# Attention denominators inverted once in 32 columns through 32x32 transposes, with the tables of beats moved

## The chip, the core and the metric

The kernel runs on one core of one Trainium2 chip. The metric is device microseconds (us) of one execution, lower is better. The engines are named as in the profile: PE (TensorE's matmuls), PEld (its weight loads), DVE (VectorE), ACT (ScalarE), POOL (GpSimd), SP (SyncE, whose queue here issues DMAs only).

## The reference

A gated cross-attention layer and a gated feed-forward layer on x (4 batches x 2048 tokens x 512 features), with a context of 154 rows for each batch. Cut to what matters:

```python
q, k, v = x_n @ Wq.T + bq, ctx @ Wk.T + bk, ctx @ Wv.T + bv    # x_n = layernorm(x); 16 heads of 32
att = softmax(q @ k.T / sqrt(32))                              # over the 154 context rows
y   = att @ v
x   = x + tanh(g_xattn) * (y @ Wo.T + bo)
h   = float_quantize(relu(layernorm(x) @ w1.T + b1), 4, 3)     # 2048 hidden features
out = float_quantize(h @ float_quantize(w2, 4, 3).T + float_quantize(b2, 5, 10), 5, 10)
x   = x + tanh(g_ffn) * out
```

The softmax's division is done last: PE sums the exponentials into denominators d and computes y without division; normalise() multiplies y by 1/d.

## The kernel before, in words

The 8192 tokens are 16 chunks of 512 (CHUNK), four chunks to a batch. Features or heads lie on the 128 partitions, tokens in the free dimension. A chunk passes through: query product (wq), row maxima of rough scores (`row_max`, L1013), scores and exponentials ("lift" on PE L644/L651, ACT L811/L814, POOL L1144), value product, normalise, output product with wo, residual and second layernorm, hidden product with w1, and ffn product with w2. The 16 heads are handled in four groups m of four heads. f16 operands are carried as a high and a low part: for a value y, ACT writes the high part (`y_hi`, L869) and POOL the rest (`y_lo`, L1161); likewise x2_hi (ACT L853) and x2_lo (POOL L1170).

**The order is written out by hand.** Each engine has its own program, a loop over "beats". A table gives the beat of every stage within its chunk (VALUE_AT = [7, 14, 21, 28] is the value product of groups 0 to 3); chunk c adds 28c (PERIOD). One period is 92.1 us in the steady part, so a beat is about 3.3 us, and three chunks are in the air at once: while one is in its scores, the one before is in its output and ffn products. Tables named ..._OWN give chunks 0 to 2 beats of their own, and single-line tables (WQ_LO, W1_LO, WO_LO, W2_LOAD and so on) give the beats of the weights' preparation. Within a beat the order of the `run(...)` lines fixes the order on the engine. An engine never goes out of order: each stage first waits on counting semaphores, and all behind it on that engine waits too.

**The value group.** `value` on PE writes d_ps: a matrix of ones, 32 wide, gives each head the sum of its exponentials, so the 32 rows of a head's block of partitions hold the same numbers. It then waits for the product before it to have left y_ps (semaphore y_scaled) and writes y_ps. Both are PSUM banks with one buffer: the next group's d_ps waits for `inverted`. `normalise` on DVE (L1035, L1038) does two halves of 256 columns, each a RECIPROCAL of the whole 128x256 half and a multiply into y32.

**The ring.** All products with 512-column results (wq "q", wo "o", w1 "h", w2 "f") write in turn to two PSUM banks, ring0 and ring1. A product waits until the one two before it has been moved out: q by DVE L1054, o by DVE L1077 (`residual`), h by ACT L836, f by DVE L1044 (first half of `finish`).

**From o to h.** `project` (PE, wo) is followed on DVE by `residual` (L1077, then statistics L1060, L1062), on POOL by the inverse root (L1179, L1182), on DVE by `ln2_apply` (L1086), then ACT x2_hi, POOL x2_lo and a transposing DMA into late_a, from which the hidden product reads. w1_lo, wo_lo and wq_lo (DVE L936) make the low parts of weights, 128x2048 at a time, in the first 170 us.

## Time and profile before

| | |
|---|---|
| three runs | 1588.94, 1587.31, 1587.6 us; median 1587.6 |
| the profiled execution | 1588.39 us, of which the span of the trace is 1586.6 |
| PE busy | 1533.4 us (97% of the span) |
| DVE, ACT, POOL busy | 951.8, 813.5, 877.2 us (60, 51, 55%) |
| DVE RECIPROCAL, L1035 | 223.4 us in 128 instructions |
| start-up, until PE is saturated | about 166 us |
| a steady chunk | 92.1 us |

An entry of the timeline gives start and duration; a row of PE bundles matmuls that follow each other, and [idle before <- releaser] names what ended a wait. The name in such a row is the buffer's without its number, so ring stands for both banks, w for w1 and w2, and y for y32.

### The profile page before, as it was taken

To read this page: it belongs to the slowest core of one execution; us is meant where nothing else is said; L and a number is where in the kernel's file an instruction comes from. 1 tells how busy PE (TensorE), PEld (TensorE's weight loads), DVE (VectorE), ACT (ScalarE), POOL (GpSimd) and SP (SyncE) were. 2 spreads that over 40 slices of the span, in tenths; PEclk is the share of its full clock that TensorE was granted. 3 is DMA by queue.
4 is the path that set the end of the run, shared out by engine and by line. 5 is a ranking of instruction groups with operands and counts; after the bars stand their busy time and mean duration, and the time that the engine had idled before them with its cause. 6 is when DMAs were issued, how large, how long until landed. Compare 5 with 4: busy or idle time off the path is not lost.

```text
span 1586.6 us, 23629 instructions
## 1 busy us (share of the span) xinstructions
PE 1533.4 (97%) x8600; PEld 695.7 (44%) x8600; DVE 951.8 (60%) x1297; ACT 813.5 (51%) x1196; POOL 877.2 (55%) x919
## 2 busy tenths in 40 slices
PE   7776999999999999999999999999999999999998
PEld 4322444444444444444444444444444444444443
DVE  7768665665746566574746657574665757445231
ACT  3674664645555464555546454545545455455421
POOL 3679465564746555574646547464654746445310
PEclk9988999999999999999999999999999999999999
DMA  8355464454544354354445434344543434333120
GB/s 338 94 152 150 128 157 122 134 116 112 109 139 94 117 136 113 101 114 138 104 119 132 115 103 119 115 103 131 135 114 104 120 113 104 100 100 86 44 54 27
DMA packets 252855, 186.70 MB, mean 118 GB/s; under 512 B 160012, under 2 KB 209476, under 8 KB 251076
## 3 DMA queue, kind: packets, MB, share of 16 engines
q1 hardware_dynamic: 252740, 185.19, 43.9%
q8 instruction: 69, 1.13, 0.3%
q14 instruction: 46, 0.38, 0.1%
HBM read 99.95 MB, written 51.59 MB: 96 GB/s over the span
## 4 chain that ended last, share of the span: by engine, by line
PE 73%; DVE 11%; POOL 7%; issue 4%; ACT 2%; DMA 2%; SPq 1%; DVEq 0%; ACTq 0%
PE ring L519 52%; PE ring L728 8%; PE m_ps L621 4%; DVE y L1035 3%; PE s_ps L651 2%; PE y_ps L679 2%; DVE bns L1060 2%; DVE resid L1077 2%; POOL pmain L1144 2%; POOL rs L1182 2%; DVE xn L1086 1%; PE d_ps L668 1%; POOL x L1170 1%; PE s_ps L644 1%; DMA yT<-in_wq_t 1%
## 5 line engine op out<-in xcount | busy, mean ns | idle before, releaser
L519 PE MATMUL ring<-late_a,w 128*128 128x512 f16 (+1 forms) x3096 | 703.1, 378 | 1.5 <-DMA late_a<-x 1.5
L519 PEld LDWEIGHTS ring<-late_a,w 128*128 128x128 f16 x3096 | 301.9, 98 | 338.8 <-issue 8.6
L1144 POOL TENSOR_TENSOR pmain<-p,pmain 128x512 f16<-128x512 f32 x256 | 304.3, 1191 | 173.8 <-ACT p L814 170.6
L836 ACT ACTIVATE late_b<-ring,b_sb,wsc 128x512 fp8e4<-128x512 f32 x256 | 199.3, 779 | 388.1 <-PE ring L519 388.1
L1013 DVE TENSOR_REDUCE smax<-m_ps 128x4 f32<-128x616 f32 x256 | 203.4, 794 | 229.6 <-PE m_ps L621 229.2
L1035 DVE RECIPROCAL y<-d_ps 128x256 f32<-128x256 f32 x128 | 223.4, 1745 | 58.6 <-PE d_ps L671 57.1
L814 ACT ACTIVATE p<-s_ps,prob_log,sc 128x512 f32<-128x512 f32 x320 | 247.9, 775 | 0.1
L728 PE MATMUL ring<-w,late_b 128*128 128x512 fp8e4 x1024 | 228.5, 379 | 5.4 <-DVE ffn L1044 3.8
L811 ACT ACTIVATE pmain<-s_ps,prob_log,sc 128x512 f16<-128x512 f32 x256 | 198.1, 774 | 2.7 <-PE s_ps L651 2.7
L1144 POOL TENSOR_TENSOR pleft<-p,pleft 128x512 f16<-128x512 f32 x64 | 76.9, 1201 | 183.3 <-ACT p L814 183.3
L519 PE MATMUL ring<-wo,yT 128*128 128x512 f16 x768 | 175.2, 382 | 0.0
L519 PE MATMUL ring<-xT,wq 128*128 128x512 f16 x720 | 167.5, 383 | 0.0
L728 PEld LDWEIGHTS ring<-w,late_b 128*128 128x128 fp8e4 x1024 | 97.7, 98 | 132.8 <-DVE ffn L1044 10.6
L853 ACT CAST x<-xn 128x512 f16<-128x512 f32 x64 | 39.5, 618 | 197.2 <-DVE xn L1086 197.2
L621 PE MATMUL m_ps<-kblk,qparts 128*128 128x308 f16 x512 | 112.0, 301 | 26.8 <-DVE smax L1013 25.5
L1156 POOL TENSOR_TENSOR qparts<-q,qparts 128x512 f16<-128x512 f32 x61 | 72.6, 1191 | 106.2 <-ACT qparts L860 106.2
L1054 DVE TENSOR_SCALAR q<-ring,sc,bias_s 128x512 f32<-128x512 f32 x61 | 49.3, 808 | 118.5 <-PE ring L519 114.1
L519 PEld LDWEIGHTS ring<-wo,yT 128*128 128x128 f16 x768 | 74.2, 98 | 92.9 <-issue 8.6
L519 PEld LDWEIGHTS ring<-xT,wq 128*128 128x128 f16 x720 | 71.0, 99 | 80.2 <-issue 3.6
L1044 DVE TENSOR_TENSOR ffn<-ring,bq 128x512 f16<-128x512 f32 x64 | 44.1, 688 | 99.5 <-PE ring L728 97.9
L651 PE MATMUL s_ps<-qstack,kcat 97*128 97x512 f16 x256 | 98.1, 385 | 2.9 <-ACT p L814 2.9
L1170 POOL TENSOR_TENSOR x<-xn,x 128x512 f16<-128x512 f32 x64 | 80.7, 1260 | 35.3 <-ACT x L853 35.3
(149 smaller groups left out, 1424.0 us busy)
## 6 DMA issues: line engine op xcount, KB each, us to landing
...
```

The lines of the kernel that those rows point to most:

```text
L519: last = pe.matmul(dst, lhs(a, k), rhs(b, k), start=(k == 0 and p == 0), stop=(k == n_k - 1 and p == 2))
L621: last = pe.matmul(m_ps[:, half, 0:HK], qparts[:, 0, m, t * P:t * P + P], kblk[:, m, half * HK:(half + 1) * HK], start=True, stop=True)
L651: pe.matmul(s_ps[unit(c, m, 1 + h) % 2][:], kcat[0:97, GH * m + h, 0:P], qstack[0:97, GH * m + h, :], start=True, stop=True).then_inc(lift ...
L728: last = pe.matmul(ring_bank("f", c, t)[:], hT[:, j, t * P:t * P + P], w2[:, j, :], start=(j == 0), stop=(j == HT - 1))
L811: nc.scalar.activation(dst, s_ps[n % 2][:], ACT.Exp, bias=prob_log[:, 0:1], scale=sc[:, 7:8])
L814: nc.scalar.activation(p32[:, n % 2, :], s_ps[n % 2][:], ACT.Exp, bias=prob_log[:, 0:1], scale=sc[:, 7:8]).then_inc(exped, 1)
L836: nc.scalar.activation(hT[:, j, :], ring_bank("h", c, j)[:], ACT.Relu, bias=b1_sb[:, j:j + 1], scale=wsc[:, j // 4, 1:2], saturate=False). ...
L1013: nc.vector.tensor_reduce(smax[:, m // 2, heads, t].rearrange("p (a h) -> p a h", a=2), score_view, AX.X, ALU.max).then_inc(maxed, 1)
L1035: nc.vector.reciprocal(y32[:, cols], d_ps[:, cols]).then_inc(inverted, 1)
L1144: nc.gpsimd.tensor_tensor(part[:, 1, :], p32[:, n % 2, :], part[:, 0, :], ALU.subtract).then_inc(prob_lo, 1)
L1156: nc.gpsimd.tensor_tensor(qparts[:, 1, m, :], q_stage(c, m), qparts[:, 0, m, :], ALU.subtract).then_inc(q_lo, 1)
L1170: nc.gpsimd.tensor_tensor(x2_16[:, t % 2, 1, :], xn2[:], x2_16[:, t % 2, 0, :], ALU.subtract).then_inc(x2_split, 1)
```

## The change

1. `normalise` is one call for each group, over all 512 columns. It transposes d_ps by 32x32 blocks into y32 (STREAM_TRANSPOSE). Since the 32 partitions of a block are equal, each block then has 32 equal columns; one column of each of the 16 blocks is inverted (128x16, new tile inv), broadcast 32 times and transposed back into y32, and one multiply of 128x512 follows. PE's next value product may write d_ps after the first transpose (semaphore den_turned) rather than after both reciprocals. The stage stands at one beat rather than two, behind `residual` and ahead of `finish`, and y_hi and y_lo at a beat earlier.
2. In the steady tables the output product, residual, second norm and x2's turn (O_AT, RESID_AT, LN2_AT, X2TURN_AT) stand a beat earlier.
3. Chunk 1's and 2's own tables and the weights' preparation get other beats: wq's low part goes from beat 4 to -1, the low parts of w1's four pieces from {16, 32, 26, 39} to {13, 26, 26, 38} (pieces 0, 2, 1, 3), the second shift of chunk 1 from 39 to 42, and so on.

```diff
-NORMAL_AT = [7, 8, 14, 15, 21, 22, 28, 29]
-SPLIT_Y_AT = [9, 16, 23, 30]
+NORMAL_AT = [7, 14, 21, 28]
+SPLIT_Y_AT = [8, 15, 22, 29]
...
-O_AT = [33, 34, 35, 36]
-LN2_AT = [34, 35, 36, 37]
-X2TURN_AT = [35, 36, 37, 38]
+O_AT = [32, 33, 34, 35]
+LN2_AT = [33, 34, 35, 36]
+X2TURN_AT = [34, 35, 36, 37]
...
-W1_LO = {0: 16, 1: 26, 2: 32, 3: 39}
+W1_LO = {0: 13, 1: 26, 2: 26, 3: 38}
...
+        inv = sb("inv", [P, CHUNK // DH], F32)
...
                 if g:
-                    pe.wait_ge(inverted, 2 * g)
+                    pe.wait_ge(den_turned, g)
...
                 if g:
-                    pe.wait_ge(y_scaled, 2 * g)
+                    pe.wait_ge(y_scaled, g)
...
             def y_hi(c, m):
-                act.wait_ge(y_scaled, 2 * group(c, m) + 2)
+                act.wait_ge(y_scaled, group(c, m) + 1)
...
-            def normalise(c, k):
-                m, half = divmod(k, 2)
-                g, cols = group(c, m), slice(half * HALF_COLS, (half + 1) * HALF_COLS)
-                if half == 0:
-                    dve.wait_ge(den_done, g + 1)
-                    if g:
-                        dve.wait_ge(y_lo_done, g)
-                    else:
-                        dve.wait_ge(q_lo, KT)
-                nc.vector.reciprocal(y32[:, cols], d_ps[:, cols]).then_inc(inverted, 1)
-                dve.wait_ge(inverted, 2 * g + half + 1)
+            def normalise(c, m):
+                g = group(c, m)
+                dve.wait_ge(den_done, g + 1)
+                if g:
+                    dve.wait_ge(y_lo_done, g)
+                else:
+                    dve.wait_ge(q_lo, KT)
+                nc.vector.transpose(y32[:], d_ps[:]).then_inc(den_turned, 1)
+                dve.wait_ge(den_turned, g + 1)
+                nc.vector.reciprocal(inv[:], y32[:].rearrange("p (b j) -> p b j", j=DH)[:, :, 0]).then_inc(inverted, 1)
+                dve.wait_ge(inverted, g + 1)
+                nc.vector.transpose(y32[:], inv[:].unsqueeze(2).to_broadcast([P, CHUNK // DH, DH])).then_inc(spread, 1)
+                dve.wait_ge(spread, g + 1)
                 dve.wait_ge(valued, g + 1)
-                nc.vector.tensor_tensor(y32[:, cols], y_ps[:, cols], y32[:, cols], ALU.mult).then_inc(y_scaled, 1)
+                nc.vector.tensor_tensor(y32[:], y_ps[:], y32[:], ALU.mult).then_inc(y_scaled, 1)
...
                 run(shift, SHIFT_AT, beat, SHIFT_OWN)
-                run(normalise, NORMAL_AT, beat)
                 run(ln2_apply, LN2_AT, beat, LN2_OWN)
...
                 run(residual, O_AT, beat, O_OWN)
+                run(normalise, NORMAL_AT, beat)
                 run(finish, FFN_AT, beat, FFN_OWN)
```

What this does to the engines' order is shown at three places. Line numbers of the changed kernel are two to four higher than those of before.

First, PE where a steady chunk's output products (wo) stand around the first value product of the next chunk. Before:

```order
L519 MATMUL ring1<-wo,yT 128x512 x12
L519 MATMUL ring0<-wo,yT 128x512 x12
L644 MATMUL s_ps1<-qstack,kcat 32x512 x4
L668 MATMUL d_ps<-pmain,ones 32x512 x8
L671 MATMUL d_ps<-pstack,ones_stack 32x512 x4
L679 MATMUL y_ps<-pmain,vmain 32x512 x12
L683 MATMUL y_ps<-pstack,vstack 32x512 x4
L519 MATMUL ring1<-wo,yT 128x512 x12
L651 MATMUL s_ps0<-qstack,kcat 128x512
L519 MATMUL ring0<-wo,yT 128x512 x12
L651 MATMUL s_ps1<-qstack,kcat 128x512
L728 MATMUL ring1<-w2,late_b 128x512 x16
```


After the change, from the same place on (a row `s_ps1`, the second lift, and the first ffn product in ring1 follow):

```order
L521 MATMUL ring0<-wo,yT 128x512 x12
L521 MATMUL ring1<-late_a,w1 128x512 x12
L623 MATMUL m_ps<-kblk,qparts 128x308 x2
L521 MATMUL ring0<-wo,yT 128x512 x12
L521 MATMUL ring1<-wo,yT 128x512 x12
L646 MATMUL s_ps1<-qstack,kcat 32x512 x4
L670 MATMUL d_ps<-pmain,ones 32x512 x8
L673 MATMUL d_ps<-pstack,ones_stack 32x512 x4
L681 MATMUL y_ps<-pmain,vmain 32x512 x12
L685 MATMUL y_ps<-pstack,vstack 32x512 x4
L521 MATMUL ring0<-wo,yT 128x512 x12
L653 MATMUL s_ps0<-qstack,kcat 128x512
```


The first output product has moved ahead of the last hidden product, the third ahead of the value product, and only the fourth is left between the value product and the ffn products; both single lifts now follow it.

Second, DVE at the same place, from the group's denominators to the last `ln2_apply` (xn2). Before:

```order
L1035 RECIPROCAL y32<-d_ps 128x256
L1038 TENSOR_TENSOR y32<-y_ps,y32 128x256
L1086 TENSOR_SCALAR xn2<-resid,mv2,rs2 128x512
L1077 SCALAR_TENSOR_TENSOR resid<-ring1,sc,resid 128x512
L1060 BN_STATS bns<-resid 128x6
L1062 BN_AGGR mv2<-bns 128x2
L1035 RECIPROCAL y32<-d_ps 128x256
L1038 TENSOR_TENSOR y32<-y_ps,y32 128x256
L1086 TENSOR_SCALAR xn2<-resid,mv2,rs2 128x512
L1077 SCALAR_TENSOR_TENSOR resid<-ring0,sc,resid 128x512
L1060 BN_STATS bns<-resid 128x6
L1062 BN_AGGR mv2<-bns 128x2
```

After, from the third `ln2_apply` to `finish`:

```order
L1090 TENSOR_SCALAR xn2<-resid,mv2,rs2 128x512
L1081 SCALAR_TENSOR_TENSOR resid<-ring0,sc,resid 128x512
L1064 BN_STATS bns<-resid 128x6
L1066 BN_AGGR mv2<-bns 128x2
L1035 STREAM_TRANSPOSE y32<-d_ps 128x512
L1037 RECIPROCAL inv<-y32 128x16
L1039 STREAM_TRANSPOSE y32<-inv 128x512
L1042 TENSOR_TENSOR y32<-y_ps,y32 128x512
L1090 TENSOR_SCALAR xn2<-resid,mv2,rs2 128x512
L1048 TENSOR_TENSOR ffn16<-ring1,bq2 128x512
L1051 SCALAR_TENSOR_TENSOR resid<-ffn16,sc,resid 128x512
```

The two half reciprocals stood one before the third and one before the last residual; the turned form stands whole behind the last residual and its statistics, just ahead of the last `ln2_apply` and of `finish`.

Third, DVE in the start-up, at the low parts of w1 (L936) around a normalise of chunk 0. Before:

```order
L936 SCALAR_TENSOR_TENSOR w1<-late_a,wsc,w1 128x2048
L1013 TENSOR_REDUCE smax<-m_ps 128x4
L1054 TENSOR_SCALAR q32<-ring0,sc,bias_s 128x512
L1070 TENSOR_SCALAR xin<-xin,mv1,rs1 128x512
L1035 RECIPROCAL y32<-d_ps 128x256
L1038 TENSOR_TENSOR y32<-y_ps,y32 128x256
L1013 TENSOR_REDUCE smax<-m_ps 128x4
L1035 RECIPROCAL y32<-d_ps 128x256
L1038 TENSOR_TENSOR y32<-y_ps,y32 128x256
```

After:

```order
L938 SCALAR_TENSOR_TENSOR w1<-late_a,wsc,w1 128x2048
L938 SCALAR_TENSOR_TENSOR w1<-late_b,wsc,w1 128x2048
L1015 TENSOR_REDUCE smax<-m_ps 128x4
L1058 TENSOR_SCALAR q32<-ring0,sc,bias_s 128x512
L1074 TENSOR_SCALAR xin<-xin,mv1,rs1 128x512
L1035 STREAM_TRANSPOSE y32<-d_ps 128x512
L1037 RECIPROCAL inv<-y32 128x16
L1039 STREAM_TRANSPOSE y32<-inv 128x512
L1042 TENSOR_TENSOR y32<-y_ps,y32 128x512
L1015 TENSOR_REDUCE smax<-m_ps 128x4
```

The row maximum that stood between the halves now follows the whole normalise, and the product for piece 2 of w1 (late_b), which before came some fifteen rows later, is ahead of it and of a row maximum.

## Rows read from the trace of the kernel before

**Rows 1.** Windows of the span: busy us of each engine (instructions), granted clock, DMA share, GB/s.

```profile
90.00:166.00 76.00, 52.44 (x278) 21.85 (x277) 61.57 (x70) 40.26 (x57) 60.45 (x56) 0.80 0.55 145
...
280.00:372.10 92.10, 91.81 (x532) 41.64 (x528) 56.93 (x76) 48.22 (x73) 53.51 (x57) 1.00 0.49 122
```

**Rows 2.** Waits over the whole span: us in total, times, longest.

```profile
PE m_ps L621 <- DVE smax L1013: 25.5, 12, 5.5
...
PEld ring L728 <- DVE resid L1077: 5.7, 14, 0.6
...
PE ring L728 <- DVE ffn L1044: 3.8, 13, 0.3
```

**Rows 3.** Timeline of PE, a steady chunk's end: start, us, what [idle before].

```profile
423.25 3.62 PE L728 MATMUL ring<-w,late_b 128*128 128x512 fp8e4 x16
426.70 0.38 PE L651 MATMUL s_ps<-qstack,kcat 97*128 97x512 f16 x1
427.07 3.63 PE L728 MATMUL ring<-w,late_b 128*128 128x512 fp8e4 x16
430.53 0.38 PE L651 MATMUL s_ps<-qstack,kcat 97*128 97x512 f16 x1
431.21 1.47 PE L728 MATMUL ring<-w,late_b 128*128 128x512 fp8e4 x6 [0.29 <-DVE ffn L1044]
```

**Rows 4.** Timeline of DVE, the same stretch.

```profile
419.15 1.74 DVE L1035 RECIPROCAL y<-d_ps 128x256 f32<-128x256 f32 x1
...
423.43 1.72 DVE L1035 RECIPROCAL y<-d_ps 128x256 f32<-128x256 f32 x1
...
426.27 0.74 DVE L1077 SCALAR_TENSOR_TENSOR resid<-ring,sc,resid 128x512 f32<-128x512 f32 x1
...
429.18 1.37 DVE L1086 TENSOR_SCALAR xn<-resid,mv,rs 128x512 f32<-128x512 f32 x1 [1.23 <-POOL rs L1182]
430.47 0.68 DVE L1044 TENSOR_TENSOR ffn<-ring,bq 128x512 f16<-128x512 f32 x1
```

**Rows 5.** Sources on DVE: count, ns min/median/max, first and last start, forms.

```profile
L1035 DVE RECIPROCAL y<-d_ps x128: 1723/1747/1758, 70.9 to 1489.3; 128x256 f32<-128x256 f32 x128
...
L1038 DVE TENSOR_TENSOR y<-y_ps,y x128: 423/424/426, 72.7 to 1491.0; 128x256 f32<-128x256 f32 x128
...
L925 DVE STREAM_TRANSPOSE amax<-fold_a x2: 211/211/211, 22.3 to 59.5; 128x32 f32<-128x32 f32 x2
...
L932 DVE RECIPROCAL rp<-pw x2: 176/182/189, 23.6 to 60.8; 128x3 f32<-128x3 f32 x1, 128x5 f32<-128x5 f32 x1
...
L1019 DVE TENSOR_SCALAR neg<-smax x32: 148/504/1175, 46.2 to 1424.6; 128x32 f16<-128x32 f32 x32
...
L1024 DVE STREAM_TRANSPOSE negT<-neg x32: 211/211/214, 46.4 to 1425.1; 128x32 f16<-128x32 f16 x32
```

**Rows 6.** Timelines of ACT and POOL in the steady stretch of rows 3.

```profile
426.91 0.77 ACT L811 ACTIVATE pmain<-s_ps,prob_log,sc 128x512 f16<-128x512 f32 x1
...
428.25 0.61 ACT L869 CAST yT<-y 128x512 f16<-128x512 f32 x1
...
429.12 1.15 POOL L1144 TENSOR_TENSOR pmain<-p,pmain 128x512 f16<-128x512 f32 x1
```

**Rows 7.** Timeline of PE, tail.

```profile
1511.94 4.26 PE L728 MATMUL ring<-w,late_b 128*128 128x512 fp8e4 x19 [0.58 <-DVE resid L1077]
```

**Rows 8.** Timeline of PE in the start-up.

```profile
113.72 0.46 PE L621 MATMUL m_ps<-kblk,qparts 128*128 128x308 f16 x2 [1.24 <-DVE smax L1013]
...
128.58 0.67 PE L621 MATMUL m_ps<-kblk,qparts 128*128 128x308 f16 x2 [3.43 <-DVE smax L1013]
...
157.55 0.67 PE L621 MATMUL m_ps<-kblk,qparts 128*128 128x308 f16 x2 [4.43 <-DVE smax L1013]
```

**Rows 9.** Source of DVE's long products of weight preparation.

```profile
L936 DVE SCALAR_TENSOR_TENSOR w<-late_b,wsc,w x1: 2686/2686/2686, 135.5 to 135.5; 128x2048 f16<-128x2048 f32 x1
L936 DVE SCALAR_TENSOR_TENSOR w<-w,wsc x1: 3287/3287/3287, 161.6 to 161.6; 128x2048 f16<-128x2048 f32 x1
```

More of the change, by code:

```diff
@@ L57 @@
 VALUE_AT = [7, 14, 21, 28]
-NORMAL_AT = [7, 8, 14, 15, 21, 22, 28, 29]
-SPLIT_Y_AT = [9, 16, 23, 30]
+NORMAL_AT = [7, 14, 21, 28]
+SPLIT_Y_AT = [8, 15, 22, 29]
 RELOAD_AT = [28, 29, 30, 31]
-RESID_AT = [30, 31, 32, 33]
-O_AT = [33, 34, 35, 36]
-LN2_AT = [34, 35, 36, 37]
-X2TURN_AT = [35, 36, 37, 38]
-HIDDEN_HALVES = {0: 39, 1: 40, 2: 41, 3: 41}
+RESID_AT = [29, 30, 31, 32]
+O_AT = [32, 33, 34, 35]
+LN2_AT = [33, 34, 35, 36]
+X2TURN_AT = [34, 35, 36, 37]
+HIDDEN_HALVES = {0: 40, 1: 40, 2: 41, 3: 42}
 HIDDEN_AT = [41, 42, 43, 45, 47, 49, 51, 52, 53, 54, 55, 56, 57, 58, 59, 60]
@@ L73 @@
 MAX_OWN = {0: [-12, -11, -10, -9, -8, -7, -6, -5, -4, -3, -2, -1, 0, 1, 2, 3], 1: [18, 19, 20, 21, 22, 23, 24, 25, 27, 29, 30, 30, 33, 34, 38, 39], 2: [46, 47, 48, 49, 50, 51, 52, 53, 54, 55, 56, 57, 58, 59, 60, 61]}
-SHIFT_OWN = {0: [-4, 4], 1: [26, 39], 2: [53, 61]}
-LN1_STAT_OWN = {1: [0, 3, 3, 6]}
-LN1_APPLY_OWN = {1: [1, 6, 9, 10]}
-XSPLIT_OWN = {1: [4, 7, 10, 11]}
-XTURN_OWN = {1: [6, 10, 14, 16]}
-Q_OWN = {1: [16, 17, 21, 27], 2: [44, 46, 50, 51]}
-STACK_OUT_OWN = {1: [19, 30], 2: [46, 53]}
-STACK_IN_OWN = {1: [24, 33], 2: [48, 59]}
-SPLIT_Y_OWN = {0: [12, 16, 24, 30]}
-RELOAD_OWN = {0: [18, 23, 28, 34]}
-RESID_OWN = {0: [29, 33, 34, 35]}
+SHIFT_OWN = {0: [-4, 4], 1: [26, 42], 2: [53, 61]}
+LN1_STAT_OWN = {1: [-1, 1, 3, 5]}
+LN1_APPLY_OWN = {1: [1, 4, 6, 7]}
+XSPLIT_OWN = {1: [3, 7, 11, 11]}
+XTURN_OWN = {1: [5, 10, 15, 15]}
+Q_OWN = {1: [16, 17, 21, 27], 2: [44, 46, 48, 50]}
+STACK_OUT_OWN = {1: [19, 27], 2: [48, 52]}
+STACK_IN_OWN = {1: [21, 31], 2: [49, 53]}
+SPLIT_Y_OWN = {0: [12, 16, 25, 30]}
+RELOAD_OWN = {0: [19, 23, 25, 28]}
+RESID_OWN = {0: [27, 32, 33, 35]}
 O_OWN = {0: [33, 35, 36, 37]}
@@ L87 @@
 HIDDEN_OWN = {0: [41, 42, 43, 45, 47, 49, 51, 52, 53, 54, 55, 56, 57, 58, 59, 60]}
-FFN_OWN = {0: [65, 66, 67, 67]}
-STORE_OWN = {0: [66, 69, 70, 72]}
+FFN_OWN = {0: [65, 66, 67, 68]}
+STORE_OWN = {0: [66, 67, 68, 69]}
 X2TURN_OWN = {0: [36, 39, 39, 39]}
-KV_STEPS = {4: [-4, -4, -3, -3], 5: [-1, 1, 1, 2], 6: [3, 5, 5, 6], 7: [5, 5, 6, 7], 8: [8, 9, 9, 10], 9: [9, 10, 10, 11], 10: [11, 11, 12, 12], 11: [14, 15, 15, 16], 12: [18, 18, 18, 19]}
+KV_STEPS = {4: [-4, -4, -3, -2], 5: [-1, 1, 1, 2], 6: [3, 5, 5, 6], 7: [5, 5, 6, 7], 8: [8, 8, 9, 9], 9: [9, 10, 10, 11], 10: [11, 12, 12, 12], 11: [14, 15, 15, 16], 12: [18, 19, 19, 19]}
 Q_STEPS = {2: [-12, -11, -10, -9], 3: [-8, -7, -6, -5]}
-KSTACK_AT = {0: -12, 1: -12, 2: -11, 3: -9, 4: -8, 5: -7, 6: -6, 7: -5}
-KEYS_OUT_AT = {0: 16}
-GATE_AT = {0: -7}
-BIAS_AT = {0: -4}
-W1_SUM = {1: -8, 2: -4, 3: -3}
-WQ_HI = {0: 0}
-WQ_LO = {0: 4}
+KSTACK_AT = {0: -12, 1: -11, 2: -10, 3: -9, 4: -8, 5: -7, 6: -6, 7: -5}
+KEYS_OUT_AT = {0: 21}
+GATE_AT = {0: -4}
+BIAS_AT = {0: -3}
+W1_SUM = {1: -9, 2: -7, 3: -2}
+WQ_HI = {0: -8}
+WQ_LO = {0: -1}
 W_FOLD = {0: 1}
-WO_HI = {0: 14}
+WO_HI = {0: 15}
 WO_LO = {0: 18}
-W1_HI = {0: 12, 1: 20, 2: 23, 3: 30}
-W1_LO = {0: 16, 1: 26, 2: 32, 3: 39}
-W2_LOAD = {0: 28, 1: 44, 2: 47, 3: 55}
-W2_PART = {0: 39, 1: 49, 2: 51, 3: 56}
+W1_HI = {0: 11, 1: 20, 2: 24, 3: 30}
+W1_LO = {0: 13, 1: 26, 2: 26, 3: 38}
+W2_LOAD = {0: 27, 1: 47, 2: 49, 3: 53}
+W2_PART = {0: 43, 1: 49, 2: 52, 3: 56}
 def build(nc, x, ctx_t, g_xattn, g_ffn, wq_t, bq, wk_t, bk, wv_t, bv, wo_t, bo, w1_t, b1, w2_t, b2, out):
@@ L244, in build @@
         lifted, exped, prob_lo = sem("lifted"), sem("exped"), sem("prob_lo")
-        den_done, inverted = sem("den_done"), sem("inverted")
+        den_done, den_turned, inverted, spread = sem("den_done"), sem("den_turned"), sem("inverted"), sem("spread")
         valued, y_scaled, y_hi_done, y_lo_done = sem("valued"), sem("y_scaled"), sem("y_hi_done"), sem("y_lo_done")
```

## The prediction, made before the changed kernel was run

> **What bounds the kernel now.** I first read the windows. In a steady chunk PE is busy 91.81 of 92.10 us at full granted clock, with DVE, ACT and POOL at 48 to 57 [rows 1]: there PE's work is the bound, and a cheaper DVE instruction is worth only the gap that it closes. In 90 to 166 us PE is busy 52.44 of 76.00, at a granted clock of 0.80, and DVE (61.57) and POOL (60.45) are the busiest: there DVE time can be time. Then the waits: what PE waits for most is DVE's row maximum, 25.5 us in 12 waits. Next come DVE's evictions ahead of the ffn products, 13 or 14 times: once in every steady chunk [rows 2]. The timeline shows this small gap. After the lift of 426.70 the second ffn product could start at 426.70 + 0.22 = 426.92 and starts at 427.07 (0.15 lost). After the lift of 430.53 the third could start at 430.75 and starts at 431.21 (0.46 lost) [rows 3]. (0.22 is the step at 2.4 GHz from one 512-column matmul to the next: 16 ffn matmuls take from 423.25 to 426.70, 3.45/16.) Together 0.61 us a chunk. I take it that 13 chunks do this.
>
> Why DVE is late there: its timeline, ahead of the eviction at 430.47, holds two half normalises (reciprocals at 419.15 and 423.43), each just before work that PE's ring needs. The last residual, which empties the bank of the second ffn product, runs at 426.27 though its product had ended before 423.25. The last ln2_apply, pushed behind it by the statistics and POOL, ends at 430.5, and only then does the first ffn product's bank get emptied [rows 3, 4].
>
> **The normalise, priced.** Before, a group costs 2 x (1.747 + 0.424) = 4.34 us of DVE [rows 5]. After, there are four instructions, of which no row of before has the size. The multiply of 128x512: an addition of that size from PSUM takes 0.68 [rows 4]. The inversion of 128x16: the short reciprocals of 3 and 5 columns take 0.18; with (1.747 - 0.182)/252 = 6.2 ns a further column, 16 columns take 0.25 [rows 5]. The transposes: 32 columns take 0.211, in f32 and f16 alike [rows 5]. Lower bound: 0.21 + 480 columns at the multiply's slope, (0.68 - 0.424)/256 = 1.0 ns, is 0.69. Upper bound: all 0.21 is paid for each of 16 blocks, 3.4. I take 0.7, since 0.15 to 0.2 is what even the smallest DVE instruction shows, so that the 0.21 is mostly a fixed part. Sum 0.7 + 0.25 + 0.7 + 0.68 = 2.35 us, 2.0 less than before; bounds 2.3 and 7.7.
>
> A row that could speak against this: the shift's small TENSOR_SCALAR swings from 148 to 1175 ns, but the transpose right behind it keeps to 211 to 214 in all 32 cases [rows 5]. So something holds the one and has not held the other, though POOL has 1.15 us instructions all about [rows 6]. By the Trainium skill ("SBUF — State Buffer", section on the two separate sides) DVE in a two-port mode and GpSimd take a shared port pair as an exclusive lock, and the loser is blocked for the other's whole instruction. If the second transpose, which goes from SBUF to SBUF, fell under it, a normalise would be up to 1.15 dearer, 3.5 us; by the rows of the 32 small transposes it stays at 2.35. The trace agrees with the rule for TENSOR_SCALAR and shows no held transpose.
>
> **The steady part.** The order shows two things. PE's third output product now ends before the value product, so that DVE's third residual is long done, and the last residual need only follow the last output product, which ends at about 422.8 (two lifts at 0.22 lie between it and 423.25). No normalise stands before it. It runs at 422.9 to 424.6 at the latest (an ln2_apply of up to 1.0 us may be ahead) against a need at 426.92: the 0.15 is gone, with over 2 us in hand. Then, on DVE: statistics 0.9 (to 425.5), the normalise 2.35 (to 427.8), ln2_apply 0.55 to 1.4 (to 428.4 to 429.2), eviction of the first ffn product 0.68 (to 429.1 to 429.9). It is needed at 430.75: the 0.46 is gone as well, with 0.9 to 1.6 in hand. All other PE work is the same in kind and count. Gain: 13 x 0.61 = 8.0 us. It can't be more than this from this cause; PE is otherwise full.
>
> The next thing that could be late is ACT: y_hi (0.61) now waits for the whole normalise at about 427.8 and stands an exp pair earlier, ahead of an x2_hi and of the exps that ran at 426.91 [rows 6]. I take this as covered, but it is the first rival.
>
> **The tail.** The last chunk has no value products after it. Its third or last residual holds the ffn product at 1511.94: 0.58 us [rows 7]. With the output products a beat earlier this falls away: 0.6.
>
> **The start-up** (five normalises of chunks 0 and 1 before PE is full). I put no term for a clock that changes. Place by place:
> - 91 to 103 us: a low part of w1 moves earlier, away from a row maximum; a short wait of PE for that maximum goes: +1.
> - 106 to 117: row maxima stand between and behind half normalises; waits such as 1.24 at 113.72 [rows 8]. 2.0 us of DVE go, PE is paced by ACT as well in part: +1.5.
> - 119 to 133: PE waits 3.43 at 128.58 [rows 8]. The 2.69 us product for late_b [rows 9] now stands ahead of this row maximum, which it delays, while the maximum no longer stands between halves. About even, up to 1 lost here; but the same 2.69 us and one 2.0 us are gone from the stretch 133 to 157, which ends in PE's wait of 4.43 at 157.55 [rows 8].
> - 157 to 167: the last 3.29 us product [rows 9] now stands ahead of a row maximum and the second shift of chunk 1, which SP must carry to the next lift. It takes back most of what 133 to 157 gave. Counted together: +1.5.
> - wq's low part at beat -1: a product of the kind of [rows 9], moved to where PE has slack on one side and a row maximum on the other; taken as 0.
>
> Sum +4. Bounds: the worst is both low parts charged in full, less a saved normalise, 2.69 - 2.0 + 3.29 = 4.0 lost. The best is all five normalises' 2.0 on PE's path, less 1 that DVE idled: 9 gained.
>
> **Sum.** 8.0 + 0.6 + 4 = 12.6. The profiled execution (1588.39) would take 1575.8. The median of the runs lies 0.8 below that execution, so I predict 1575 us.
>
> **Rivals.**
> 1. *ACT's new place for y_hi eats the steady gain.* ACT waits until 427.8, then y_hi 0.61, x2_hi 0.6, which itself waits for the last ln2_apply (428.4 to 429.2), and the two exps of 0.77 that free the bank of the lift of 430.53 [rows 3, 6]. They end between 429.8 and 431.3, against a need at about 430.5: 0 to 0.9 us a chunk lost instead of 0.61. For it: everything on ACT waits in order, and the new wait is for four instructions. Against it: the middle of the estimates has it just in time. At 0.6 a chunk only tail and start-up are left: 1587.6 - 4.6, about 1583.
> 2. *The start-up gives more.* Each us that DVE is earlier in 106 to 157 carries, as the row maxima's 25.5 us are mostly there. A gain of 10: 1569. Against it: both low parts now stand before row maxima.
> 3. *The transposes are dear: slower.* The margin of 0.9 to 1.6 behind the normalise is used up if it costs over 3.3 to 4.0 us; at 2 x 0.46 us more than the gap is back, so that it decides from some 1.3 us per transpose on. If each is held for one POOL instruction (0.7 + 1.15 = 1.85), the normalise is 4.65, the eviction ends at 431.4 to 432.2, and 0.7 to 1.4 us a chunk are lost instead of 0.61: 0 to +10 us, and the start-up's gain is gone: about 1594. At 3.4 each (7.7) it is 4.5 to 5 a chunk, over 1635. Against it: no transpose of the trace took over 0.214 us. Only the second held, once: a normalise of 3.5, the eviction at 430.3 to 431.1, 0 to 0.35 us a chunk lost, a gain of 3 to 8 in the steady part, about 1579. (The lock of the page named above, if it took in transposes, would do this second thing.)
> 4. *No change.* The gap of 0.61 returns as another wait (rival 1 in full), and the start-up's reordered low parts cost the 4 they might bring: 1587.
>
> **How the numbers follow.** Forecast (steady gap closed, start-up 0 to 8): 0.50, its own range 1571 to 1580. Rival 1: 0.20 (1580 to 1585). Rival 2: 0.12. Rival 3: 0.09. Rival 4: 0.09. 0.2% is 3.2 us, about what a measurement can tell from no change of this kernel. Faster than 1584.4: 0.50 + 0.12 + most of rival 1 = 0.80; within: 0.11; slower than 1590.8: 0.09. The range runs from the start-up's better half (1587.6 - 8.6 - 9 = 1570, and 3 lower, since a DVE that is ahead also starts the weights' preparation and the DMAs behind it earlier, which the bound of 9 leaves out) to rival 1's and part of rival 4's end: 1567 to 1586.5.
>
> **What would show it.** Right: in a steady chunk no wait of an ffn product for DVE, a chunk of 91.5 us in place of 92.1, STREAM_TRANSPOSE of 128x512 at 0.7 us, normalise instructions summing to 2.35, the waits for row maxima down from 25.5 to about 20. Wrong: transposes over 1.3 us; a wait of a lift for ACT's exps at the end of each chunk; a start-up (until PE is full) not near 162 us; waits at the shift or the lift behind the last low part of w1.

## The result, and the profile after

The changed kernel takes 1583.34 us (median of 10 runs, 1581.32 to 1586.63), the kernel before 1587.34 (10 runs, 1586.45 to 1588.94): ratio 0.9975, 95% interval [0.9965, 0.9984]. It is faster by 4.0 us, where 12.6 were forecast: the time lies in the forecast's range of 1567 to 1586.5, the gain is a third of it. The profiled execution took 1584.49 us with a span of 1582.7, against 1588.39 and 1586.6, so that its traces differ by 3.9 us.

The windows of the kernel after, in the start-up and in a steady chunk, answer to [rows 1]:

```profile
90.00:166.00 76.00, 49.97 (x279) 21.26 (x281) 51.73 (x69) 39.48 (x56) 59.45 (x56) 0.80 0.55 151
...
280.00:372.10 92.10, 92.10 (x532) 41.88 (x531) 47.47 (x76) 48.33 (x72) 53.63 (x56) 1.00 0.46 122
```

PE is now busy the whole of the steady chunk (92.10 of 92.10). DVE has dropped from 56.93 to 47.47 us: 7.9 of the 9.5 are the four normalises, the rest other DVE instructions that ran shorter. Almost nothing of it is time. In the start-up DVE is down from 61.57 to 51.73 and PE still does less in the same 76 us (49.97 against 52.44). The granted clock is 0.80 in both windows, but not in their parts: in 90 to 140 us it was 0.76 before and is 0.80 after, in 140 to 166 us it was 0.87 and is 0.80.

The sources of the four instructions of the normalise on DVE (against [rows 5]):

```profile
L1035 DVE STREAM_TRANSPOSE y<-d_ps x64: 697/707/717, 72.7 to 1483.9; 128x512 f32<-128x512 f32 x64
...
L1037 DVE RECIPROCAL inv<-y x64: 252/254/255, 73.4 to 1484.7; 128x16 f32<-128x16 f32 x64
...
L1039 DVE STREAM_TRANSPOSE y<-inv x64: 711/711/712, 73.7 to 1485.0; 128x512 f32<-128x512 f32 x64
...
L1042 DVE TENSOR_TENSOR y<-y_ps,y x64: 691/691/693, 74.5 to 1485.7; 128x512 f32<-128x512 f32 x64
```

0.71 + 0.25 + 0.71 + 0.69 = 2.36 us, with minimum and maximum within 0.02 of the median in 64 cases each. The prediction's price was 2.35.

The waits over the whole span (against [rows 2]):

```profile
PE m_ps L623 <- DVE smax L1015: 22.6, 14, 4.8
...
PEld ring L521 <- DVE resid L1081: 6.0, 14, 0.4
...
PE ring L730 <- ACT late_b L838: 0.9, 1, 0.9
```

The 13 waits of ffn products for DVE are gone, and so is the tail's wait of [rows 7]. The waits for row maxima went from 25.5 to 22.6 us only.

The timelines of PE and DVE at the place of [rows 3, 4]; the value product now stands later in the order, so that this place comes a little later in the span:

```profile
425.12 0.60 PE L653 MATMUL s_ps<-qstack,kcat 97*128 97x512 f16 x2
425.55 3.62 PE L730 MATMUL ring<-w,late_b 128*128 128x512 fp8e4 x16
429.01 0.38 PE L653 MATMUL s_ps<-qstack,kcat 97*128 97x512 f16 x1
429.23 3.62 PE L730 MATMUL ring<-w,late_b 128*128 128x512 fp8e4 x16
```

```profile
425.69 0.74 DVE L1081 SCALAR_TENSOR_TENSOR resid<-ring,sc,resid 128x512 f32<-128x512 f32 x1
...
427.30 0.70 DVE L1035 STREAM_TRANSPOSE y<-d_ps 128x512 f32<-128x512 f32 x1
...
429.67 0.54 DVE L1090 TENSOR_SCALAR xn<-resid,mv,rs 128x512 f32<-128x512 f32 x1
430.14 0.68 DVE L1048 TENSOR_TENSOR ffn<-ring,bq 128x512 f16<-128x512 f32 x1
```

PE goes from the two lifts at 425.12 to the first ffn product (425.55), 3.46 us later to the lift and 0.22 us later to the second ffn product, without a gap. The last residual (425.69) frees its bank at 426.43, 2.8 us ahead of 429.23. The first ffn product's bank is empty at 430.82; the third ffn product will need it at 432.91.

**Where the time came from.** The two traces can be laid on each other at the value products, whose start is PE's row L668 (L670 after). Value product 5 is chunk 1, group 1, and so on. At 5 the changed order has put half a hidden product (1.28 us) behind this place, which the last column takes out; at the other places here PE has the same work behind it.

| value product | before, us | after, us | after less before | same work |
|---|---|---|---|---|
| 0 | 70.03 | 69.72 | -0.31 | -0.31 |
| 2 | 102.12 | 99.52 | -2.60 | -2.60 |
| 4 | 140.40 | 137.46 | -2.94 | -2.94 |
| 5 | 167.06 | 165.65 | -1.41 | -0.13 |
| 7 | 209.04 | 208.96 | -0.08 | -0.08 |
| 9 | 256.76 | 259.38 | +2.62 | +2.62 |
| 13 | 348.87 | 351.05 | +2.18 | +2.18 |
| 17 | 441.03 | 442.72 | +1.69 | +1.69 |
| 21 | 533.12 | 534.38 | +1.26 | +1.26 |
| 61 | 1453.58 | 1450.92 | -2.66 | -2.66 |
| end of span | 1586.6 | 1582.7 | -3.9 | -3.9 |

So the changed kernel was 2.9 us ahead at 140 us, about as forecast to this point, lost 2.8 between 140 and 167, lost 2.7 more between 209 and 259, and then gained 0.43 to 0.49 in each of the chunks shown, 5.3 to value product 61, and 1.2 behind it: 0.7 in the tail, near the forecast's 0.6, and 0.5 that was not foreseen (PE's wait for POOL ahead of value product 62, 1.14 us before, is 0.62).

The loss between value products 4 and 5 can be read off PE row by row:

| PE between value products 4 and 5 | before, us | after, us |
|---|---|---|
| a lift's wait for ACT's p | 1.82 | 2.15 |
| wait for a row maximum | 4.43 | 4.78 |
| first 24 matmuls of a hidden product | 4.62 | 5.29 |
| wait for late_a | 1.49 | 1.78 |
| a lift's wait for the shift rows | none | 1.16 |

Together 12.36 and 15.16, the 2.8 us. Rows after, of PE and of DVE, and the one of DVE before that answers to the latter:

```profile
155.26 0.67 PE L623 MATMUL m_ps<-kblk,qparts 128*128 128x308 f16 x2 [4.78 <-DVE smax L1015]
155.73 5.29 PE L521 MATMUL ring<-late_a,w 128*128 128x256 f16 x24
...
165.44 0.40 PE L646 MATMUL s_ps<-qstack,kcat 97*32 97x512 f16 x4 [1.16 <-DMA qstack<-negT]
```

```profile
151.46 1.37 DVE L1090 TENSOR_SCALAR xn<-resid,mv,rs 128x512 f32<-128x512 f32 x1 [2.84 <-POOL rs L1186]
```

```profile
153.75 1.37 DVE L1086 TENSOR_SCALAR xn<-resid,mv,rs 128x512 f32<-128x512 f32 x1 [1.47 <-POOL rs L1182]
```

The row maximum stands on DVE behind this ln2_apply, the next residual and its statistics. DVE is idle ahead of it in both kernels, waiting for POOL's inverse root, so that time saved on DVE doesn't shorten PE's wait here. The experiments below tell what lengthened it.

The loss between 209 and 259 us is PE's wait of 2.52 us at 226.35 and 0.53 at 220.85, less the chunk's usual gain. Timelines of ACT, POOL, DVE and PE there:

```profile
216.37 1.91 ACT L803 ACTIVATE w<-resid 128x2048 fp8e4<-128x2048 f32 x1 [1.44 <-DMA resid<-in_w_t]
...
219.51 0.61 ACT L871 CAST yT<-y 128x512 f16<-128x512 f32 x1
...
220.80 1.15 POOL L1165 TENSOR_TENSOR yT<-y,yT 128x512 f16<-128x512 f32 x1
221.91 1.27 POOL L1180 TENSOR_TENSOR resid<-resid,gbo 128x512 f32<-128x512 f32 x1
...
223.54 0.55 POOL L1186 TENSOR_TENSOR rs<-rs,minus_half 128x1 f32<-128x1 f32 x1
...
224.13 1.37 DVE L1074 TENSOR_SCALAR xin<-xin,mv,rs 128x512 f32<-128x512 f32 x1 [6.12 <-POOL rs L1186]
...
226.35 0.42 PE L623 MATMUL m_ps<-kblk,qparts 128*128 128x308 f16 x2 [2.52 <-DVE smax L1015]
```

ACT waits 1.44 us for the load of w2's last piece and converts it for 1.9. y_hi (219.51) comes late behind that. POOL has y_lo (220.80) and a reload's addition, and only then the inverse root of chunk 3's first norm (223.54). DVE waits 6.12 us for that root, and the row maximum that frees m_ps stands behind it. In the kernel before, ACT converted this piece without a wait (215.16), and y_lo stood behind this inverse root (220.00 the root, 221.63 y_lo).

### The profile page after: what moved, and what is told of

Its sections match the earlier page's. It is cut to its first block, busy times and chain, and to the rows that moved or that the text cites. A ratio compares the mean times of both kernels' runs of the same rounds, so it can differ in the third digit from the quotient of the medians.

```text
span 1582.7 us, 23565 instructions
## 1 busy us (share of the span) xinstructions
PE 1530.0 (97%) x8600; PEld 695.8 (44%) x8600; DVE 805.9 (51%) x1297; ACT 814.3 (51%) x1196; POOL 879.5 (56%) x919
## 4 chain that ended last, share of the span: by engine, by line
PE 91%; POOL 3%; DVE 2%; DMA 1%; ACT 1%; issue 1%; SPq 0%; ACTq 0%; DVEq 0%
PE ring L521 61%; PE ring L730 14%; PE m_ps L623 4%; PE s_ps L653 3%; PE y_ps L681 3%; PE d_ps L670 2%; PE s_ps L646 1%; POOL pmain L1148 1%; PE y_ps L685 1%; PE d_ps L673 1%; DMA yT<-in_wq_t 1%; PE ring L581 1%; POOL yT L1165 0%; DVE w L938 0%; POOL qparts L1160 0%
## 5 line engine op out<-in xcount | busy, mean ns | idle before, releaser
L623 PE MATMUL m_ps<-kblk,qparts 128*128 128x308 f16 x512 | 112.6, 302 | 26.5 <-DVE smax L1015 22.6
L1169 POOL TENSOR_TENSOR x<-xin,x 128x512 f16<-128x512 f32 x60 | 71.6, 1194 | 49.8 <-ACT x L847 49.8
L862 ACT CAST qparts<-q 128x512 f16<-128x512 f32 x61 | 37.7, 618 | 114.1 <-DVE q L1058 114.1
```

The costliest lines, as they stand in the source:

```text
L623: last = pe.matmul(m_ps[:, half, 0:HK], qparts[:, 0, m, t * P:t * P + P], kblk[:, m, half * HK:(half + 1) * HK], start=True, stop=True)
L1169: nc.gpsimd.tensor_tensor(x16[:, t % 2, 1, :], xin[:, t, :], x16[:, t % 2, 0, :], ALU.subtract).then_inc(x_split, 1)
```

## The experiments

Each was timed against the kernel before in the same set of runs on one chip (medians of 1587.2 to 1587.6 us). "Form" is the turned normalise, "steady tables" are those for all chunks, "start tables" the ..._OWN ones and those for the weights.

**The form alone.** The kernel before with the changed `normalise` and its semaphores; tables and order of before, the whole normalise at the beat and place of the old second half.

```diff
-NORMAL_AT = [7, 8, 14, 15, 21, 22, 28, 29]
+NORMAL_AT = [8, 15, 22, 29]
```

> Only the turned normalise on the tables of before (whole at the beat and the place of the old second half). Theory A, the steady gain comes from DVE's shorter chain whatever the order: DVE is 4.34 - 2.35 = 2 us earlier at the last residual and at the ffn eviction, 0.6 us a chunk are closed, and a start-up without the new tables gains 0 to 4: 1576 to 1581. Theory B, it is the new order that closes the gap: 1584 to 1588, with DVE waits of about 0.5 us ahead of the ffn products still there.

Measured: 1586.40 us (11 runs), ratio 0.999 [0.9982, 0.9999]. Theory B: the steady gap is all there, and value products 9 to 57 are as far apart as before to 0.1 us. The trace is 2.7 us ahead at value product 5, all that the form alone gives, where the medians of the runs differ by 1.2 only. Timelines of DVE and PE in the same chunk as [rows 3, 4] (some 3 us earlier in the span):

```profile
413.19 1.48 DVE L1090 TENSOR_SCALAR xn<-resid,mv,rs 128x512 f32<-128x512 f32 x1 [0.72 <-POOL rs L1186]
...
417.51 1.37 DVE L1090 TENSOR_SCALAR xn<-resid,mv,rs 128x512 f32<-128x512 f32 x1 [1.23 <-POOL rs L1186]
...
422.78 0.55 DVE L1090 TENSOR_SCALAR xn<-resid,mv,rs 128x512 f32<-128x512 f32 x1
...
426.15 1.37 DVE L1090 TENSOR_SCALAR xn<-resid,mv,rs 128x512 f32<-128x512 f32 x1 [1.23 <-POOL rs L1186]
427.44 0.68 DVE L1048 TENSOR_TENSOR ffn<-ring,bq 128x512 f16<-128x512 f32 x1
...
427.50 0.38 PE L653 MATMUL s_ps<-qstack,kcat 97*128 97x512 f16 x1
428.18 1.68 PE L730 MATMUL ring<-w,late_b 128*128 128x512 fp8e4 x7 [0.29 <-DVE ffn L1048]
```

The counterpart of 417.51 in the kernel before:

```profile
421.36 0.55 DVE L1086 TENSOR_SCALAR xn<-resid,mv,rs 128x512 f32<-128x512 f32 x1
```

DVE is 2 us a group lighter and idles where it had no wait before: 1.23 us ahead of the ln2_apply at 417.51, and 1.23 at 426.15 as before, each time for POOL's inverse root. The last ln2_apply ends at the same place relative to PE as before, the eviction is at 427.44 and PE loses its 0.46 us at 428.18. From the first of the four ln2_apply to the last are 12.96 us, and were 13.05. The first and the last of these three steps are set by a round: ln2_apply, x2_hi on ACT, x2_lo on POOL, inverse root on POOL (in order behind x2_lo), next ln2_apply (417.51 - 413.19 = 4.3 us and 426.15 - 422.78 = 3.4). In the middle step the whole normalise still holds the ln2_apply at 422.78, 0.8 us behind the end of POOL's root (421.92). And the ln2_apply at 417.51 takes 1.37 us where its counterpart took 0.55. So what the shorter normalise saves comes back as waits in the round and as a longer ln2_apply.

**The tables alone.** The new kernel with the old reciprocals and multiplies, both halves one after the other at the new place.

```diff
-NORMAL_AT = [7, 14, 21, 28]
+NORMAL_AT = [7, 7, 14, 14, 21, 21, 28, 28]
```

> The new tables and the new place, with the old reciprocals and multiplies (both halves one after the other at the new beat). Theory A: the normalise of 4.34 us stands ahead of the last ln2_apply and the ffn eviction, which comes at 431 to 432 where 430.75 is needed: 0.3 to 1.2 us a chunk, and the start-up loses: 1588 to 1598. Theory B: faster than before, 1580 to 1584.

Measured: 1611.11 us (5 runs), ratio 1.015 [1.0136, 1.0164]. Slower, as theory A had it, by more than its range, and by another wait. Timelines of ACT and PE:

```profile
436.93 0.62 ACT L869 CAST yT<-y 128x512 f16<-128x512 f32 x1 [3.87 <-DVE y L1038]
437.45 0.61 ACT L853 CAST x<-xn 128x512 f16<-128x512 f32 x1
...
439.46 0.39 PE L651 MATMUL s_ps<-qstack,kcat 97*128 97x512 f16 x1 [1.34 <-ACT p L814]
```

ACT waits 3.87 us for the normalise, then comes x2_hi and only then the exponentials; PE's lift waits 1.34 us for them in each chunk. It is the mechanism of rival 1, with the 4.34 us normalise: PE waits for ACT's p 23.2 us in 16 times. With y at its new beat the new tables need the short form.

**The output stages alone a beat earlier**, with old reciprocals at their old beats, once with the new HIDDEN_HALVES and once without.

```diff
-RESID_AT = [30, 31, 32, 33]
-O_AT = [33, 34, 35, 36]
-LN2_AT = [34, 35, 36, 37]
-X2TURN_AT = [35, 36, 37, 38]
+RESID_AT = [29, 30, 31, 32]
+O_AT = [32, 33, 34, 35]
+LN2_AT = [33, 34, 35, 36]
+X2TURN_AT = [34, 35, 36, 37]
```

> The kernel before with the output product, residual, second norm and x2's turn a beat earlier, and the old reciprocals at their old beats. Theory A, the steady gap is closed by this order alone, whatever the normalise costs: 1580 to 1583, a steady period of 91.6 to 91.7 us. Theory B, order and short normalise are both needed: 1586 or more, with another wait in each chunk in place of the old one.

> The kernel before with only the output stages a beat earlier and the hidden halves where they were. Theory A, the later hidden halves cost 1.2 us in the start-up (the wait for the shift rows at 167 us): 1582 to 1583. Theory B, they cost nothing: 1583.8, as with them moved.

Measured: 1583.78 us (10 runs), ratio 0.9977 [0.9968, 0.9986], and 1583.18 (5 runs), 0.9964 [0.995, 0.9977]. The first is 0.8 above theory A's range, but its mechanism is there: the order closes the gap with the old form, and a steady chunk is about 0.55 us shorter. The second pair of theories isn't told apart by the runs (0.6 us), but by the profiles: with the new halves a lift waits 1.07 us for the shift rows at 167.60, with the old ones it doesn't. It is the same between the new kernel (1.16 us at 165.44) and the one with the halves alone put back (below; no such wait): half a hidden product less stands ahead of this lift. Two steady windows of the latter run:

```profile
280.00:372.10 92.10, 92.10 (x532) 42.08 (x531) 55.67 (x77) 48.17 (x72) 54.16 (x57) 1.00 0.48 121
372.10:464.20 92.10, 91.63 (x530) 41.67 (x528) 55.57 (x77) 48.18 (x72) 53.32 (x57) 1.00 0.45 117
```

The first is full, the second has lost 0.47: there PE waits for a row maximum at 405.91. It is the only steady chunk that does, and with the short form and y at the old beats none does. This wait is all that the short form is worth in the steady part, once the order is right. As much speed as the whole change has (4.0 us) comes from moving four stages by a beat.

**The new kernel with the old start tables.**

> The new kernel with the tables of before for chunks 0 to 2 and the weights. Theory A, the new start-up tables cost about 3 us (the stall at 220 to 226 us): 1578 to 1581 and no PE wait for the row maximum there. Theory B, they gain and the new y place costs: 1584 to 1588.

Measured: 1585.08 us (11 runs), ratio 0.9981 [0.9973, 0.999]. In theory B's range: the stall for a row maximum is there all the same (1.76 us at 225.59), so the start tables alone don't cause it. The new kernel has 1.7 us less, but the intervals of the two ratios overlap: that the new start tables gain isn't shown here, only that they cost no 3 us.

**w2's loads and conversions at the old beats**, in the new kernel.

> The new kernel with only the loads and conversions of w2 at the beats of before. Theory A, the stall at 220 to 226 us comes from ACT's conversion of w2's last piece, whose load lands late (8.1 us): with it gone 1580 to 1581, and the runs lie closer together. Theory B, it comes from y_lo standing a beat earlier on POOL, ahead of an inverse root: the stall of 2 to 3 us stays, 1583.

Measured: 1592.42 us (6 runs), ratio 1.003 [1.0018, 1.0041]. Both theories missed by 9 us and more: the stall of 2.52 stayed (at 236.55), and the old beats brought a new one. Nor could the run tell the two theories apart, since of the last piece it moves only the load (beat 53 to 55): the conversion stands at beat 56 in both tables, and ACT still waited 1.39 us for the load. SP and PE:

```profile
196.01 0.35 SPq L466 DMA_DIRECT2D resid<-in_w_t  x1
...
212.37 2.55 SPq L396 DMA_DIRECT2D qstack<-negT  x4
...
216.31 0.62 PE L646 MATMUL s_ps<-qstack,kcat 97*32 97x512 f16 x4 [4.89 <-DMA qstack<-negT]
```

The shift rows (qstack<-negT) are sent at 212.37, where the new kernel sends them at 202.83, since SP stood from 173 us on at the load of w2's third piece, which must wait until ACT has converted the second (194.09 to 195.99) and is issued at 196.01, with the stacking of q queued behind it. PE waits 4.89 us for the shift rows. The trace is 10.2 us longer than the new kernel's, 5.3 more than this wait. The granted clock is 0.70 in 160 to 172 us and 0.51 in 215 to 222, where the new kernel has 0.96 and 1.00; how the 5.3 divide isn't shown. The load's old beat (47, the conversion's is 49) fits only with the old places of SP's other work.

**y a beat later**, for chunk 1's last group only, and throughout.

```diff
-SPLIT_Y_OWN = {0: [12, 16, 25, 30]}
+SPLIT_Y_OWN = {0: [12, 16, 25, 30], 1: [36, 43, 50, 58]}
```

> The new kernel with one entry changed: y of chunk 1's last group is split a beat later, as before. Theory A, the stall of 2.5 us at 226 us is POOL's inverse root behind this y_lo: 1580 to 1581, no PE wait for the row maximum at 220 to 230 us. Theory B, it is ACT's conversion of w2: 1583 to 1584, the wait stays.

> The new kernel with y_hi and y_lo at the steady beats of before (9, 16, 23, 30). Theory A, the earlier y place is no part of the gain: the same steady period of 91.7 us or 0.1 less, and the stall at 226 us gone as well: 1579 to 1581. Theory B, the earlier y is needed by the output products: slower than the new kernel, 1584 or more.

Measured: 1580.80 us (5 runs), ratio 0.9962 [0.995, 0.9974], and 1582.23 (5 runs), 0.9963 [0.9951, 0.9974]. The first has theory A's time, though a wait stays; the second is 1.2 above its theory A's range and nearer to it than to theory B. POOL in the first of them:

```profile
219.33 0.55 POOL L1186 TENSOR_TENSOR rs<-rs,minus_half 128x1 f32<-128x1 f32 x1
...
220.97 1.33 POOL L1165 TENSOR_TENSOR yT<-y,yT 128x512 f16<-128x512 f32 x1
```

The inverse root (219.33) is now ahead of y_lo (220.97), and PE's wait of 2.52 is one of 0.93. Not all of the difference is y's place, since in this profile ACT didn't wait for w2's last load either. The profiles side by side:

| kernel | y of this group | ACT's wait for the load | PE's wait for the row maximum |
|---|---|---|---|
| before; the form alone | old beat | none | none |
| y later for one group; y later throughout; the fastest (below) | old beat | none | 0.93; 0.92; 0.93 |
| the fastest with w1's old beats (below) | old beat | 0.97 | 1.92 |
| new kernel, old start tables | new beat | none | 1.76 |
| halves alone put back (below); new kernel | new beat | 1.17; 1.44 | 2.52; 2.52 |

So 0.9 us come with the new steady tables whatever y does, 0.8 with y's new beat and 0.8 to 1.0 with a late load (the wait of 0.53 us at 220.85 is in the profiles with a late load and y at its new beat only). No experiment says why it is late in some kernels and not in others (in the new kernel it lands 8.1 us after its issue, in the run with one entry changed 6.1).

y's place costs at 148 to 155 us as well. There the lift's wait for p and the wait for the row maximum are 6.9 us together in the three profiles with y at the new beat and the new start tables, and 5.4 to 5.7 in the three with y at the old one: 1.3 us. On POOL y_lo (148.25) stands ahead of x2_lo and the inverse root (150.88) that the ln2_apply at 151.46 waits for. The other half of the story is what doesn't change: the wait for the row maximum there is 4.42 or 4.43 us before, with the form alone, with the order alone and in the fastest, whatever a normalise costs.

In every steady chunk of the new kernel y's place works in the same way, but less. Timelines of POOL, DVE and PE:

```profile
404.14 1.16 POOL L1165 TENSOR_TENSOR yT<-y,yT 128x512 f16<-128x512 f32 x1
...
406.87 0.55 POOL L1186 TENSOR_TENSOR rs<-rs,minus_half 128x1 f32<-128x1 f32 x1
...
407.46 1.37 DVE L1074 TENSOR_SCALAR xin<-xin,mv,rs 128x512 f32<-128x512 f32 x1 [2.79 <-POOL rs L1186]
...
409.33 0.38 PE L653 MATMUL s_ps<-qstack,kcat 97*128 97x512 f16 x1
409.69 0.42 PE L623 MATMUL m_ps<-kblk,qparts 128*128 128x308 f16 x2
```

y_lo at 404.14, inverse root at 406.87, DVE waits 2.79, and the product of the rough scores (m_ps) starts 0.36 us after the lift where 0.22 is the step: 0.14 lost. With y at the old beats throughout a chunk gains 0.54 to 0.62 on the kernel before, not 0.43 to 0.49.

**Sums.** The new kernel in all three. The first has the start tables of before with the normalise of chunks 0 and 1 at beat 8 and so on, and y of these chunks at its old beats; the second also puts y and hidden halves back; the third has in addition the normalise at beat 8 throughout.

```diff
-NORMAL_AT = [7, 14, 21, 28]
+NORMAL_AT = [8, 15, 22, 29]
```

> New normalise and new steady tables; the start-up tables of before, and in chunks 0 and 1 normalise and y at their beats of before (8 and 9, and so on). If start-up and steady part add up, the start-up gives the 2.9 us of the normalise alone and the steady part 0.49 a chunk and 0.6 in the tail: 1587.5 - 2.9 - 6.9 = 1577.7. If they don't add up, the stall for the row maximum comes back in the start-up: 1581 to 1585.

> Steady tables of the new kernel but y at the beats of before and the hidden halves at the beats of before; start-up tables of before, normalise of chunks 0 and 1 at their old second-half beats. Theory A, start-up gain of the short normalise (2.3 us) and steady gain (0.57 a chunk, as with the later y) add up: 1587.4 - 2.3 - 7.4 - 0.6 = 1577 to 1579. Theory B, the steady tables cost 2 to 3 us in the start-up whatever y does: 1580 to 1582.

> As the run before it, but the normalise at the second-half beat (8, 15, 22, 29) throughout, behind the residual of its beat. Theory A, the place of normalise within a beat or two is free once it is short: within 1 us of the run before it. Theory B, the shorter way from the normalise to y_hi costs ACT time and PE waits for exponentials: 2 us or more slower than that run.

Measured: 1582.41 us (5 runs), ratio 0.9968 [0.9957, 0.998]; 1580.63 (5 runs), 0.9952 [0.9939, 0.9964]; and 1596.76 (5 runs), 1.0055 [1.0041, 1.0069]. The first and second add up only in part, 2 to 5 us short of the sum. Both sums took the form's gain in the start-up (2.9 and 2.3 us) from single traces, while its runs give 1.2. The third showed "the place is free once the normalise is short" to be false: 16 us for one beat. Its waits:

```profile
PE m_ps L623 <- DVE smax L1015: 35.7, 26, 5.5
...
PEld ring L730 <- DVE ffn L1048: 9.1, 14, 0.7
```

The ffn waits are back (the normalise is again ahead of the first eviction and behind the last ln2_apply), and one wait for a row maximum a chunk has been added (26 in place of 13), 0.79 us in a steady chunk, the maximum standing directly behind the normalise.

**New start tables, y and hidden halves at the old beats.** The new kernel with the two lines put back.

```diff
-SPLIT_Y_AT = [8, 15, 22, 29]
+SPLIT_Y_AT = [9, 16, 23, 30]
-HIDDEN_HALVES = {0: 40, 1: 40, 2: 41, 3: 42}
+HIDDEN_HALVES = {0: 39, 1: 40, 2: 41, 3: 41}
```

> The new kernel with y_hi and y_lo at the steady beats of before and the hidden halves at theirs. Theory A, the new start-up tables are worth 1 to 2 us, the later y 3 us: 1579 to 1580.5. Theory B, the new start-up tables are worth nothing or less: 1582 and slower than the first run of this set.

Measured: **1578.64 us** (5 runs, 1576.20 to 1580.88), ratio 0.994 [0.9927, 0.9953]. This is the fastest, 8.5 us under the kernel before and 4.7 under the changed one, and a little below theory A's range. The parts seen above are of this size: y's place 0.13 us in each of 12 steady chunks (1.6), 0.8 at 226 us and 1.3 at 148 to 155, the later halves 1.1, together 4.8 (an estimate from single traces). Against the sum with the old start tables (1580.63) the new start tables have 2.0 us less, with overlapping intervals.

**The hidden halves alone, and w1's parts at the old beats** in that fastest version.

> The new kernel with only the hidden halves at the beats of before. Theory A, the later halves cost the new kernel 1 to 3 us in 157 to 175 us (half a product less ahead of the wait for the shift rows, and a low clock behind it): 1580.5 to 1582.5. Theory B, all of the 4.7 us between the new kernel and the run with later y and old halves are the y place: 1583 to 1584.

> The fastest version so far (new kernel, y and hidden halves at the beats of before) with the high and low parts of w1 at the beats of before. Theory A, the low parts moved ahead of row maxima cost time, as the prediction had it: 1575 to 1577. Theory B, moving them ahead is a gain, since DVE is then free for the rows behind: 1579.5 to 1583. No difference: within 1 us of 1578.6.

Measured: 1582.18 us (7 runs), ratio 0.9966 [0.9954, 0.9977], and 1579.62 (5 runs), 0.9947 [0.9934, 0.996]. The first lies in the range of theory A, but 1.2 us under the new kernel is within what runs scatter: the medians don't settle it. Its profile has no wait for the shift rows. The second: no difference that 5 runs show. The low parts moved ahead of row maxima neither cost nor give more than about a microsecond.

## Why the prediction was wrong

- **The price of the normalise** (2.35 us, 2.0 saved a group) was right: 2.36. The transposes at 0.7 were right, and POOL held none of them: 697 to 717 and 711 to 712 ns in 64 cases each. The lock in the Trainium skill ("SBUF — State Buffer", the two separate sides) is stated there for DVE in a two-port mode or with two SBUF inputs, and names no transpose; by this trace it doesn't reach these.
- **The start-up** (+4) is the step that failed: up to value product 9 the trace lost 3.1 us (2.6, and a chunk's gain of 0.5 is already in it). Up to 140 us it was about right. The +1.5 for the stretch behind it rested on DVE's lighter load shortening PE's wait of 4.43 us for a row maximum. That wait isn't made by DVE's work but by the round through ACT and POOL: it stays at 4.42 or 4.43 with the short form, and is 4.78 in the changed kernel.
- **Two table entries got no term at all.** y a beat earlier was looked at on ACT alone; on POOL it stands ahead of an inverse root, and that costs about 3.7 us (1.6 in the steady chunks, 0.8 and 1.3 in the start-up). The later hidden halves aren't in the prediction; they cost the 1.1 us wait for the shift rows. With both put back the kernel is 4.7 us faster. The stretch 209 to 259 us was taken as free of changes because PE is busy there; but the inverse root of the next chunk's norm, y_lo and w2's last load and conversion meet in it.
- **The steady part** (8.0) had the right place and too large a size: both waits of the ffn products are gone, 0.61 us a chunk, but 0.43 to 0.49 arrive, 5.8 in all (5.3 and the first chunk's 0.5). Most of the rest is the new wait of 0.14 behind y_lo.
- **The reason given for the gap** (two half normalises, "each just before work that PE's ring needs") was wrong in its weight. With the form alone the gap stays, with the order alone it closes. Of [rows 4] the prediction read the two reciprocals and named POOL only in passing; the 1.23 us for POOL's inverse root at 429.18 were the sign of the round.
- **The tail** (0.6): right.
- **The low parts of w1**, which set the lower bound of the start-up: no difference could be told. A sign of being wrong that the prediction named, a wait behind the last low part of w1, did come (1.16 us at 165.44), but not from it: with the halves put back and the low part where it is, the wait is gone.
- **Rival 1** (ACT) named the right engine for the old form (1.34 us a chunk, seen with the tables alone) and not for the new one: y_hi at 429.79 delays no lift. That its figure of about 1583 us is the measured one is luck.

Sum of the profiled execution: +2.6 at value product 9, -5.3 in the steady part and -1.2 behind it: -3.9, against -12.6. Of the 8.7 us between them the start-up has 7.1 and the steady part 2.2; 0.5 came unforeseen the other way.

What stays open in 140 to 167 us is the time of the hidden products and the wait for late_a, about 1 of the 2.8 us. The first 24 matmuls took 4.62 us at a granted clock of 0.59 before and 5.29 at 0.52 after. How much that varies is seen in the fastest version and in the one with w1's old beats, whose programs differ little there. PE's hidden products after the wait for late_a read:

```profile
160.86 2.78 PE L521 MATMUL ring<-late_a,w 128*128 128x256 f16 x24 [3.47 <-DMA late_a<-x]
```

```profile
161.48 5.28 PE L521 MATMUL ring<-late_a,w 128*128 128x256 f16 x24 [3.62 <-DMA late_a<-x]
```

and the windows 160 to 168 us of the two:

```profile
160.00:168.00 8.00, 7.14 (x68) 4.25 (x69) 2.37 (x4) 4.23 (x6) 1.54 (x2) 1.00 0.18 56
```

```profile
160.00:168.00 8.00, 6.52 (x48) 4.07 (x52) 0.07 (x1) 1.44 (x2) 0.08 (x1) 0.57 0.21 52
```

In one the granted clock is 1.00 and the 24 matmuls take 2.78 us, in the other it is 0.57 (part of the window at 1.2 GHz) and they take 5.28. PE had waited 3.47 and 3.62 us just before. The runs of the two kernels differ by 1.0 us only (1578.64 and 1579.62), so one profile can't say whether a table brings such a difference of 2.5 us. Nor was the later start of the hidden halves shown to cause it.
